# The third layer's scan: every fourth value product moves from VectorE to GpSimd, and TensorE's head sums run one step behind

## The reference

```python
q = jnp.concatenate([q * c, q * s_], axis=-1)
k = jnp.concatenate([k * c, k * s_], axis=-1)
def step(S, inp):
    qt, kt, vt, lt = inp
    S = jnp.exp(lt)[..., None] * S + kt[..., None] * vt[..., None, :]
    o = jnp.einsum('bhe,bhev->bhv', qt, S)
    return (S, o)
_, o = jax.lax.scan(step, S0, seq)      # over the 2048 tokens
g = o * jax.nn.sigmoid(x @ wg1 @ wg2)   # then an RMS norm by head and @ wo
```

## Time and profile before

| | |
|---|---|
| Median of 3 runs | 1258.63 us (1257.43 to 1260.14) |
| The profiled execution, its own time | 1258.89 us |
| Its span, first to last instruction | 1257.1 us |
| Busy in the span: PE / DVE / ACT / POOL | 79% / 73% / 51% / 48% |
| Granted TensorE clock, mean | 0.920 of full speed |
| The 32 steps, from the first value product to the last head sums | 241.85 to about 357.8 us |

### The profile page before, as it was taken

How to read it: one execution, slowest core, us unless ns; L and a number is a source line. 1 busy time by engine, 2 the same in 40 slices (tenths; PEclk the granted TensorE clock), 3 DMA queues, 4 the chain that set the end, 5 groups by cost and what they waited for, 6 DMA issues and landing times.

```text
span 1257.1 us, 12629 instructions
## 1 busy us (share of the span) xinstructions
PE 988.2 (79%) x3048; PEld 560.2 (45%) x3048; DVE 921.3 (73%) x1229; ACT 638.2 (51%) x1157; POOL 599.4 (48%) x432
## 2 busy tenths in 40 slices
PE   5849888388878984599999999876676776675896
PEld 2314343133326723488888888432222222224684
DVE  4684895999977568466666666587989998955564
ACT  4744657300054483255555555776555555453455
POOL 3010275566630033277777777303656565623572
PEclk9979899599998996699999999987989998997899
DMA  2000300000020000476666666000000000000661
GB/s 72 1 0 0 111 0 15 0 0 1 0 59 0 1 16 7 92 156 152 146 142 155 151 147 156 3 0 1 0 0 0 0 0 0 1 13 15 149 153 34
DMA packets 18639, 61.22 MB, mean 49 GB/s; under 512 B 2560, under 2 KB 12416, under 8 KB 12800
## 3 DMA queue, kind: packets, MB, share of 16 engines
q1 hardware_dynamic: 18608, 60.86, 20.7%
HBM read 59.15 MB, written 1.70 MB: 48 GB/s over the span
## 4 chain that ended last, share of the span: by engine, by line
PE 48%; DVE 34%; issue 6%; ACT 5%; POOL 4%; DMA 2%; DVEq 1%; SPq 0%; POOLq 0%; ACTq 0%
PE ps L351 46%; DVE g L1378 5%; DVE g L1177 4%; DVE tmp L1177 4%; DVE y L1628 3%; DVE g L1628 2%; ACT rstd L759 2%; ACT g L759 2%; DVE resid L1177 2%; DVE parts L1317 2%; DVE parts L1177 2%; POOL g L1164 2%; DVE g L1585 1%; POOL sq L1068 1%; DMA g<-coef_scratch 1%
## 5 line engine op out<-in xcount | busy, mean ns | idle before, releaser
L351 PE MATMUL ps<-parts 128*128 128x512 f32 x1800 | 449.8, 408 | 34.1 <-DVE g L1177 10.0
L351 PEld LDWEIGHTS ps<-parts 128*128 128x128 f32 x1800 | 345.1, 194 | 137.8 <-DVE parts L1177 17.9
L759 ACT ACTIVATE g<-ps 128x512 f32<-128x512 f32 (+4 forms) x310 | 183.0, 597 | 314.7 <-PE ps L351 285.1
L1107 POOL TENSOR_TENSOR parts<-g,parts 128x512 fp32r<-128x512 f32 x168 | 217.6, 1295 | 156.2 <-ACT parts L759 152.2
L1164 POOL TENSOR_TENSOR g<-g 128x1024 f32<-128x1024 f32 x64 | 150.3, 2353 | 137.9 <-ACT g L759 134.9
L351 PE MATMUL ps<-g,arena 128*128 128x512 f32 (+1 forms) x328 | 164.9, 645 | 62.0 <-POOL g L1151 23.5
L1177 DVE TENSOR_TENSOR ps<-g,ps 128x512 f32<-128x512 f32 x168 | 116.9, 696 | 112.6 <-PE ps L351 90.7
L759 ACT ACTIVATE parts<-g 128x512 fp32r<-128x512 f32 (+2 forms) x252 | 126.3, 534 | 30.9 <-DVE g L1177 15.8
L351 PEld LDWEIGHTS ps<-g,arena 128*128 128x128 f32 (+1 forms) x328 | 62.3, 201 | 162.9 <-issue 61.0
L1177 DVE TENSOR_TENSOR g<-ps,g 128x512 f32<-128x512 f32 x160 | 110.7, 692 | 32.7 <-DMA g<-coef_scratch 14.9
L1068 POOL TENSOR_TENSOR sq<-resid 128x512 f32<-128x512 f32 x32 | 35.9, 1122 | 198.5 <-DVE resid L1177 185.0
(11 more groups left out here) (172 smaller groups left out, 1067.7 us busy)
## 6 DMA issues: line engine op xcount, KB each, us to landing
g<-coef_scratch SPq DMA_DIRECT2D x80, 512.0 KB, 6.2
g<-in_moe_dram SPq DMA_DIRECT2D x42, 192.0 KB, 4.9
g<-in_rope_dram SPq DMA_DIRECT2D x1, 2048.0 KB, 8.5
arena<-in_weights_dram SPq DMA_DIRECT2D x1, 1348.5 KB, 5.8
arena<-in_weights_dram SPq DMA_DIRECT2D x1, 1028.5 KB, 4.8
g<-in_x_dram SPq DMA_DIRECT2D x4, 256.0 KB, 4.0
out_dram<-g SPq DMA_DIRECT2D x4, 256.0 KB, 2.5
arena<-in_weights_dram SPq DMA_DIRECT2D x1, 838.0 KB, 6.9
```

What stands on the lines that cost most here:

```text
L351: return nc.tensor.matmul(o, lhsT, rhs, start=start, stop=stop, **kw)
L759: return nc.scalar.activation(o, i, func, **kw)
L1107: pv.tensor_tensor(hid_lo[:, cols(c)], g[:, 6, (c % 2) * N:(c % 2 + 1) * N], hid_hi[:, cols(c)].bitcast(F32), ALU.subtract).then_inc(s["hl ...
```

## The change

For the steps k = 3, 7, ..., 31 the value product is done by GpSimd. As GpSimd doesn't read PSUM here, ScalarE first copies the bank to SBUF (`v_copy(k)`, two halves of `sq` in turn), signalled by `v_copied`. GpSimd does the product of step k + 3 just behind its query product of step k (`features_in`), signalled by `in_pool`. TensorE's head sums of step k - 1 are issued behind the spread of step k + 3, so they lag by one step more than before. VectorE waits for `in_pool` before the scans of a step whose product GpSimd made, and has one more wait in its own products (`st_ready`), and a new semaphore, `kr_ready`, tells GpSimd that the turned keys are there. The diff has first the helpers, then TensorE, ScalarE (`act`), GpSimd (`pool`) and VectorE (`dve`, `tt`).

```diff
+        def of_pool(k):
+            return (k + 1) // 4
+        def of_dve(k):
+            return k + 1 - of_pool(k)
+        def v_copy(k):
+            return sq[:, k // 4 % 2 * N:(k // 4 % 2 + 1) * N]
...
                 if k >= 3:
-                    pe.wait_ge(s["vb_used"], k - 2)
+                    if (k - 3) % 4 == 3:
+                        pe.wait_ge(s["v_copied"], of_pool(k - 3))
+                    else:
+                        pe.wait_ge(s["vb_used"], of_dve(k - 3))
...
-            for c in range(CHUNKS):
-                for e in range(8):
-                    k = 8 * c + e
-                    if k + 3 < 8 * CHUNKS:
-                        spread_v(k + 3)
-                    pe.wait_ge(s["qm_ready"], k + 1)
-                    for r in range(2):
-                        last = mm(ps[:, c, :], W(2, "head_sum", e * 128, e * 128 + 128),
...
+            def sum_heads(k):
+                e, c = k % 8, k // 8
+                pe.wait_ge(s["qm_ready"], k + 1)
+                for r in range(2):
+                    last = mm(ps[:, c, :], W(2, "head_sum", e * 128, e * 128 + 128),
...
+            for k in range(8 * CHUNKS):
+                if k + 3 < 8 * CHUNKS:
+                    spread_v(k + 3)
+                if k:
+                    sum_heads(k - 1)
+            sum_heads(8 * CHUNKS - 1)
...
+            for k in range(3, 8 * CHUNKS, 4):
+                act.wait_ge(s["vb_bank"], k + 1)
+                if of_pool(k) > 2:
+                    act.wait_ge(s["in_pool"], of_pool(k) - 2)
+                f(v_copy(k), ps[:, v_bank(k), :], ACT.Copy).then_inc(s["v_copied"], 1)
...
+                    def features_in(k):
+                        pool.wait_ge(s["v_copied"], of_pool(k))
+                        pv.tensor_tensor(two_of(0, 11, k), g[:, 6:8, cols(k // 8)],
+                                         v_copy(k).unsqueeze(1).to_broadcast([P, 2, N]), ALU.mult)\
+                            .then_inc(s["in_pool"], 1)
+                    pool.wait_ge(s["kr_ready"], 1)
...
+                            k = 8 * c + e + 3
+                            if k % 4 == 3 and k < 8 * CHUNKS:
+                                features_in(k)
...
-                chain(tt(G(7, c), G(4, c), G(11, c)))
-            chain.wait()
+                last = tt(G(7, c), G(4, c), G(11, c))
+                if c + 1 < CHUNKS:
+                    chain(last)
+            last.then_inc(s["kr_ready"], 1)
+            dve.wait_ge(s["kr_ready"], 1)
...
                 dve.wait_ge(s["vb_bank"], k + 1)
+                if k >= 4:
+                    dve.wait_ge(s["st_ready"], k - 3)
...
-                if k + 1 < 8 * CHUNKS:
+                if k + 1 < 8 * CHUNKS and (k + 1) % 4 != 3:
                     inputs(k + 1)
                 e, c = k % 8, k // 8
-                dve.wait_ge(s["vb_used"], k + 1)
+                if k % 4 == 3:
+                    dve.wait_ge(s["in_pool"], of_pool(k))
+                else:
+                    dve.wait_ge(s["vb_used"], of_dve(k))
```

More of the change, by code:

```diff
@@ L149, in sandwich @@
             q_bank2 k_bank2 g1_bank g2_bank k2_ready sigq_ready q_used g1_ready gate_ready
-            m_ready md_ready me_ready s_ready rs_ready vb_bank vb_used st_ready
+            m_ready md_ready me_ready s_ready rs_ready vb_bank vb_used v_copied in_pool kr_ready st_ready
             qm_ready qm_used og_ready nrm_ready wo_bank setup2
@@ L490, in _ @@
                 spread_v(k)
-            for c in range(CHUNKS):
-                for e in range(8):
-                    k = 8 * c + e
-                    if k + 3 < 8 * CHUNKS:
-                        spread_v(k + 3)
-                    pe.wait_ge(s["qm_ready"], k + 1)
-                    for r in range(2):
-                        last = mm(ps[:, c, :], W(2, "head_sum", e * 128, e * 128 + 128),
-                                  g[:, 2, (2 * (e % 2) + r) * N:(2 * (e % 2) + r + 1) * N],
-                                  e == 0 and r == 0, e == 7 and r == 1)
-                    last.then_inc(s["qm_used"], 1)
+            def sum_heads(k):
[3 more added lines that the diff above has]
+                    last = mm(ps[:, c, :], W(2, "head_sum", e * 128, e * 128 + 128),
+                              g[:, 2, (2 * (e % 2) + r) * N:(2 * (e % 2) + r + 1) * N],
+                              e == 0 and r == 0, e == 7 and r == 1)
+                last.then_inc(s["qm_used"], 1)
+            for k in range(8 * CHUNKS):
[4 more added lines that the diff above has]
+            sum_heads(8 * CHUNKS - 1)
             variance("rms", 0, W(2, "head_mean"))
```

## The result

The changed kernel takes 1247.55 us in the median of 6 runs (1246.05 to 1250.05), where the kernel before, timed beside it, took 1259.39 (1257.43 to 1261.97). The ratio is 0.9906, with a 95% interval of 0.9889 to 0.9922: 11.8 us less, 9.8 to 14.0. The forecast was 1251.0 with a range of 1248.0 to 1255.5, a gain of 7.6. The direction was right, and the time is 0.45 us under the range. The profiled execution took 1246.34 us, its span is 1244.5.

What follows compares the result with a forecast made beforehand. VectorE's own queue was taken to bound the third layer's scan. The terms 8.96 + 0.78 - 1.30 - 0.8 = 7.6 us took the median of 1258.63 to 1251.0 us, range 1248.0 to 1255.5.

Steps and rivals of the forecast that it cites:

- Value products off VectorE: Third layer's scan: eight value products leave VectorE's full queue, each giving back 1.12 us, a gain of 8.96 us.
- the stall: Step 4 of the scan: VectorE's value product waited behind half-clock head sums; the new order removes this, gain 0.78 us.
- The same eight on GpSimd: Scan, groups of four steps: GpSimd needs 11.80 us against VectorE's 12.80, so 1.00 us of slack and no cost.
- Head sums a step behind: TensorE's order in the scan: the spread no longer stands behind head sums; gain 0.78 us, tightest point 0.3 us to spare.
- The tail: End of the scan: GpSimd's last query product starts 1.37 us behind the last scans, where before some 0.07; loss 1.30 us.
- the clock: Last head sums of the scan: TensorE's gap may lower its clock, costing 0 to 1.9 us; 0.8 taken.
- All moved together.: Behind the scan: last head sums, gate product and the rest of the layer move together, with no change of their own.
- rival D: Whole gain, no low clock at the tail, backlog partly absent: 8.4 to 9.7 us, 1249 to 1250.2; with the forecast 0.71.
- A: Scan: GpSimd becomes the bound, its products stretched up to 4.1 us by VectorE's reads; 52 us longer, 1310; chance 0.06.
- B: Scan: GpSimd's group just balances at 2.65 to 2.78 us an instruction; 1255 to 1258; chance 0.06 at its balance.
- C: Scan: small waits on VectorE, late arrivals or low clock cut the gain; 1254 to 1256; 0.17 with the milder B.

Runs made afterwards that it cites:

- lag_only: The kernel before with only TensorE's new order (head sums of step k-1 behind the spread of step k+3), all value products on VectorE; ratio 0.9992.
- value_twice: The changed kernel with every value product of GpSimd done twice, the first time into an unused buffer; 1281.04 us, ratio 1.0152.
- offload_only: The changed kernel with TensorE's old order, head sums of step k ahead of the spread of step k+4; ratio 0.9969.
- last_on_dve: The changed kernel with the value product of step 31 left on VectorE, so GpSimd has seven; median 1250.0 us, ratio 0.9919.
- decay_in_sbuf: The changed kernel with the decay of the scans kept in SBUF in place of PSUM; 1307.35 us, ratio 1.0385.
- after_late06: The changed kernel with one idle VectorE product (about 0.60 us) in front of the last chunk's gate product; ratio 0.9914.
- before_late27: The kernel before with five idle VectorE products (about 2.7 us) in front of the last chunk's gate product; ratio 1.0028.
- after_again: The changed kernel, unchanged, run again for a second trace; ratio 0.9919.
- after_pad8: The changed kernel with 8 tiny GpSimd memsets behind the third layer's scan; ratio 0.9915.
- after_pad24: The changed kernel with 24 tiny GpSimd memsets behind the third layer's scan; ratio 0.9912.
- after_pad56: The changed kernel with 56 tiny GpSimd memsets behind the third layer's scan; ratio 0.9900.
- last_on_dve_pad1: The changed kernel with step 31's value product left on VectorE and one tiny GpSimd memset behind the scan; 1249.67 us, ratio 0.9917.
- before_again: The kernel before, unchanged, run again for a second trace; ratio 1.0003.
- before_pad8: The kernel before with eight tiny GpSimd memsets behind the third layer's scan, where GpSimd is idle; ratio 0.9985.
- before_padall: The kernel before with idle instructions where engines wait: 8 GpSimd memsets, 14 ScalarE copies and 13 VectorE memsets; ratio 0.9981.

## Why the prediction was right, and where it failed

**Value products off VectorE, 8.96, and the stall, 0.78.** Right. From the first value product to the end of the last scans it is 101.5 us after (242.16 to 343.65) for 111.4 (241.85 to 353.28), 9.9 less where 9.7 was summed. lag_only gives the stall alone, 0.9.

**The same eight on GpSimd at no cost, by 1.00 us of slack.** Right: 2349 ns, no idle time on VectorE, 1.1 us left in a group. What was not seen is how steep the cost is once that slack is used up. value_twice was priced as GpSimd's excess alone, at 11 us, and cost 31.8.

**Head sums a step behind.** It was booked with the 0.78 us of the one stall only. By offload_only it is worth the whole scan's gain: without the lag 0.1 us of 7.5 is left. The prediction's text had the reason, the spread that stands behind head sums; it priced it for the old scan alone. Its total holds, since the change has both parts, but its split between them does not.

**The tail, 1.30, and the clock, 0.8.** The mechanism was right. The clock fell, and GpSimd's last product waited 1.42 us for it, where 0.8 was booked; last_on_dve, whose gap is 1.49 us, has neither the fall nor the wait. GpSimd's own lateness is the other 1.1 us. From the end of the last scans to the gate product it is 7.01 us for 4.53 before, so the tail cost about 2.5 us for 2.1. The scan's sum was 7.6, measured in the trace 7.46. That these agree so closely is in part luck, as 0.2 us more off VectorE and 0.4 more in the tail offset each other in part.

**"All moved together."** This is the step that failed: the rest of the kernel was taken as a block that keeps its length, with a change of nothing. The text named a loss there as a way to be wrong, and no gain. It doesn't keep its length. The whole gain was 11.8 us where 7.6 was forecast, and the scan is right to 0.2 us. The rest lies in the later layers, most of all in the seventh, which takes 313.6 us in the mean of the four traces with GpSimd's late start and 310.4 in that of six of the changed kernel and its variants. It costs up to 5 us more or less by what its chunk starts do to TensorE's clock. Over 15 traces (without value_twice and decay_in_sbuf), 45 such starts, the cost has three levels: nothing (12 times), 1.2 to 1.6 us (25) and 2.2 to 2.4 (8). Two things sort the sum of a trace: how its clock changes lie against the layer, marked here by the distance from the layer's start to the first fall, and GpSimd's late or early start.

| first fall behind the layer's start, us | late start: cost, us | early start: cost, us |
|---|---|---|
| 27.6 | 6.3 (before) | 1.5, 1.4 (changed kernel, after_late06) |
| 27.8 to 28.2 | 5.3, 5.3 (before_late27, lag_only) | 2.7 in each of five (offload_only, after_again, after_pad8, after_pad24, after_pad56) |
| 28.4 to 28.7 | | 5.4, 5.3 (last_on_dve, last_on_dve_pad1) |
| 29.1 to 29.3 | 2.9 (before_again) | 3.4, 3.4 (before_pad8, before_padall) |

So the early start goes with 4.8 and 2.6 us less in two of these places and with 0.5 more in another, and it doesn't protect last_on_dve. Four traces with the late start cost 4.9 in the mean, the two padded ones of the old scan 3.4, and six of the changed kernel and its variants 2.3. These are single traces, and the sixth layer varies too (343.0 to 345.2 us), so only the medians price an edit.

The gain is made up, as far as is known, of 7.5 us in the scan, about 1.9 with GpSimd's early start (0.9985 and 0.9981 measured) and about 1 that is argued only, from 3.4 less 2.3 us in the traces, and may be placement: 10.4. The changed kernel and its four copies with idle instructions or none have ratios of 0.9900 to 0.9919, 10.2 to 12.6 us. That the eight instructions bring the 0.3 us of the early start is shown. That the early start acts through the clock is argued from the table, and why they bring it stays open.

**The range.** Its lower end, 1248.0, was rival D less 1 us for the spread of medians. Nothing in it stood for a gain in later layers. The runs shown before already spread over 2.7 us. That the time fell just under the range and not just into it is chance: four repeats and variants of the changed kernel have medians of 1248.0 to 1248.5. That the gain is larger than forecast is not, as all of them gained 10 us or more.

**The rivals.** A's contention is real in a kernel that is not this one, decay_in_sbuf. Its size came out there (1307 us for 1310), but by luck: VectorE's scans grew, and GpSimd did not become the bound. Here the decay's place in PSUM keeps it away. This agrees with the Trainium skill (SBUF — State Buffer, Who interferes with whom), by which two SBUF inputs on VectorE contend with GpSimd's reads and one doesn't. B and C did not occur. D's time was undercut, though not by its mechanism: the clock did fall at the tail.

## What to carry to other kernels

When one engine's queue is shortened by moving work to a second engine, look at what a third one waits for in its written order: here the same move is worth 7.5 us with TensorE's head sums a step behind, and nothing without. Slack per group of steps can be a cliff where a late producer also lowers TensorE's clock: here 18.9 us of added products cost 31.8. And a layer with thin pieces on TensorE can differ by 3.4 us between two executions of the same kernel. So a gain of a fraction of a per cent is to be read layer by layer, in more than one trace of each kernel, before it is credited to the edit.

## What the hardware showed that was not expected

- Eight idle GpSimd instructions in a pause made the first product of a loop 500 us later start 0.3 us sooner, and the kernel 1.9 us faster (0.6 to 3.0).
- The piece of work at a chunk start was equally thin before and after (2.46 and 2.44 us in 4.5), yet TensorE's clock fell behind it in one trace and stayed at 1.00 in the other.
- With both operands in SBUF beside GpSimd's products the scans took up to 3302 ns for 1250, and GpSimd's value products 3266 for 2349: both engines lose, VectorE more.
- In the changed scan GpSimd ran five 128x1024 products a group at 91% busy (63.36 us in 270 to 340) with the same 2.35 us for each as at 66% (19.94 in 30 before).
